# One table of node sums instead of two, with each store issued behind its predecessor

## What is computed

```python
# layer 0, per edge e and head h
scores = einsum(Q[dst], K[src] + 0.2 * rel[edge_type]) / 8
w = segment_softmax(scores, dst)
agg = segment_sum(w * V[src], dst)          # 12,500 x 4 x 64
x = layernorm(x + layernorm(agg @ Wo + bo + x) * gamma + beta)
# layer 1, edges and one self loop per node
xp = x @ W;  alpha = leaky_relu(a_src[src] + a_dst[dst])
w = segment_softmax(alpha, dst)
agg = segment_sum(xp[src] * w, dst)
out = layernorm(x + elu(agg + bias))
```

## Time and profile before

| | us |
|---|---|
| median of 3 runs | 4471.25 |
| lowest, highest | 4469.44, 4473.03 |
| profiled execution, span | 6181.0 |

### The profile page before, as it was taken

How to read it: one execution, slowest core, us unless ns; L and a number is a source line. 1 busy time by engine, 2 the same in 40 slices (tenths; PEclk the granted TensorE clock), 3 DMA queues, 4 the chain that set the end, 5 groups by cost and what they waited for, 6 DMA issues and landing times. The chain is left out here.

```text
span 6181.0 us, 164556 instructions
## 1 busy us (share of the span) xinstructions
PE 4261.5 (69%) x50798; PEld 2746.6 (44%) x50798; DVE 3295.8 (53%) x10527; ACT 2576.2 (42%) x6781; POOL 3049.7 (49%) x3229
## 2 busy tenths in 40 slices
PE   7958878777778787778786555555555555555554
PEld 4634444444444444444443444444444443444443
DVE  3235555555555555555554455555555555555555
ACT  2323344444444444444343444444444444444444
POOL 1245555545555555555452555555555555555553
PEclk9989999999999999999997666656566566565666
DMA  7856676666666666666664555555555555555554
GB/s 224 282 163 191 185 189 186 186 186 185 186 187 183 186 186 187 185 186 186 184 185 114 145 153 156 152 151 153 152 153 153 150 152 149 154 152 152 154 150 123
DMA packets 820553, 1055.91 MB, mean 171 GB/s; under 512 B 458633, under 2 KB 632338, under 8 KB 820464
## 3 DMA queue, kind: packets, MB, share of 16 engines
q0 software_dynamic: 225072, 730.03, 42.9%
q1 hardware_dynamic: 594078, 324.02, 20.6%
q10 hardware_dynamic: 1314, 0.99, 0.1%
HBM read 919.46 MB, written 133.59 MB: 170 GB/s over the span
## 5 line engine op out<-in xcount | busy, mean ns | idle before, releaser
L766 POOL DMA_INDIRECT typed_rows<-kv,typed_index x1563 | 1491.3, 954 | 1470.8 <-remote 570.5
L1298 POOL DMA_INDIRECT plain_rows<-xp,plain_index x1563 | 1486.0, 951 | 1359.5 <-remote 536.1
L875 PE MATMUL typed_p_s<-typed_kt,typed_q 64*32 64x416 f32 x4168 | 835.7, 549 | 336.6 <-issue 289.7
L997 DVE CUSTOM_DVE_ANT_0 typed_weight<-typed_p_s,typed_far 128x416 f32<-128x416 f32 x521 | 308.3, 592 | 1113.6 <-PE typed_p_s L875 1080.8
L1400 PE MATMUL plain_p_o<-plain_rows,plain_weight_t 128*32 128x65 f32 x16672 | 630.5, 296 | 331.5 <-issue 310.7
L1433 DVE SCALAR_TENSOR_TENSOR plain_p_s<-plain_p_s,plain_a_dst,plain_damped 128x416 f32<-128x416 f32 x521 | 342.3, 657 | 865.9 <-ACT plain_damped L1553 475.1
L1389 PE MATMUL plain_p_s<-all_cst,plain_rows 128*128 128x128 f32 x2084 | 546.2, 395 | 346.0 <-issue 319.6
L1375 PE MATMUL plain_p_w<-all_cst,plain_weight 128*128 128x128 f32 x1563 | 437.5, 404 | 431.6 <-issue 286.0
L1400 PEld LDWEIGHTS plain_p_o<-plain_rows,plain_weight_t 128*32 128x32 f32 x16672 | 459.2, 154 | 556.6 <-issue 516.7
L1167 ACT ACTIVATE typed_weight<-typed_weight,typed_col 128x416 f32<-128x416 f32 x521 | 334.7, 642 | 806.6 <-issue 549.7
L1389 PEld LDWEIGHTS plain_p_s<-all_cst,plain_rows 128*128 128x128 f32 x2084 | 406.0, 210 | 463.6 <-issue 437.6
(11 more groups left out here) (191 smaller groups left out, 6936.5 us busy)
## 6 DMA issues: line engine op xcount, KB each, us to landing
typed_match<-match SPq DMA_DIRECT2D x131, 208.0 KB
plain_match<-match SPq DMA_DIRECT2D x131, 208.0 KB
agg<-qkv_zero SPq DMA_DIRECT2D x98, 264.0 KB
typed_agg<-agg SPq DMA_DIRECT2D x98, 264.0 KB
plain_agg<-agg SPq DMA_DIRECT2D x98, 264.0 KB
kv<-qkv_kv SPq DMA_DIRECT2D x98, 258.0 KB
typed_kinds<-match SPq DMA_DIRECT2D x131, 192.0 KB
typed_rows<-kv,typed_index POOLq DMA_INDIRECT x1563
```

What stands on the lines that cost most here:

```text
L766: pool.indirect_dma_start(rows[:, r, j, :], None, k.kv, bass.IndirectOffsetOnAxis(ap=index[:, g, at:at + 1], axis=0)).then_inc(rows_in[r], 16)
L875: last = pe.matmul(p_s[at:at + TN, 0:SLOTS], q[own, m, :, h // 2], kt[own, h // 2, lo:lo + SLOTS], start=True, stop=True, tile_position=(H ...
L1298: pool.indirect_dma_start(rows[:, r, j, :], None, k.xp, bass.IndirectOffsetOnAxis(ap=index[:, g, at:at + 1], axis=0)).then_inc(rows_in[r], 16)
```

## The change

The table has one half. Tiles store to it in turn; from the second tile on, SyncE waits, behind the wait for the tile's result, until the store of the tile before has landed, and then issues the store. Rows that a tile doesn't own are so overwritten by the next tile. Nothing is zeroed but the 44 rows of nodes that don't exist (one DMA ahead of the loop). `load` fetches one half, 132 KB. VectorE's addition is gone in both layers. In layer 1 the block is fetched straight into `both`, and counts on the semaphore of the block's other load (`own_in`); its `load` now waits for `part_ready` of three blocks back instead of `joined` of the block before.

```diff
-        self.agg = dram("agg", (2, NP, HEADS, AG))
+        self.agg = dram("agg", (NP, HEADS, AG))
...
-            def clear(t):
-                sp.dma_start(k.agg[:, bass.ds(t.n * P, P)].rearrange("a n h c -> n a (h c)"), zero[:]).then_inc(zero_out, 16)
...
-            in_turn(sp, (0, load), (4, store), (0, clear))
-            sp.wait_ge(zero_out, 16 * ROWS)
+            sp.dma_start(k.agg[N:NP].rearrange("n h c -> n (h c)"), zero[0:NP - N]).then_inc(zero_out, 16)
+            in_turn(sp, (0, load), (4, store))
+            sp.wait_ge(zero_out, 16)
...
@@ put_out of layer 0, and the same lines in layer 1 @@
                 sp.wait_ge(result_ready, t.n + 1)
                 sp.sem_inc(slot_free, 1)
-                sp.dma_start(k.agg[t.slot(2), bass.ds(node, TN)].rearrange("n h c -> h n c"), result[:, m]).then_inc(result_out[m], 16)
+                if not t.known_below(1):
+                    before = t.back()
+                    sp.wait_ge(result_out[before.slot(4)], before.use(4) * 16 + 16)
+                    sp.sem_inc(slot_free, 1)
+                sp.dma_start(k.agg[bass.ds(node, TN)].rearrange("n h c -> h n c"), result[:, m]).then_inc(result_out[m], 16)
...
@@ load of layer 0 @@
-                sp.dma_start(agg[:], k.agg[:, bass.ds(b.n * P, P)].rearrange("a n h c -> n a (h c)")).then_inc(agg_in, 16)
+                sp.dma_start(agg[:], k.agg[bass.ds(b.n * P, P)].rearrange("n h c -> n (h c)")).then_inc(agg_in, 16)
...
@@ join of layer 0 @@
-                v.tensor_tensor(agg[:, 0], agg[:, 0], agg[:, 1], ALU.add).then_inc(joined, 1)
-                v.wait_ge(joined, b.n + 1)
...
@@ load of layer 1 @@
-                if not b.known_below(1):
-                    sp.wait_ge(joined, b.n)
-                sp.dma_start(agg[:], k.agg[:, bass.ds(b.n * P, P)].rearrange("a n h c -> n a (h c)")).then_inc(agg_in, 16)
+                if not b.known_below(GROUP):
+                    sp.wait_ge(part_ready, b.n - GROUP + 1)
+                sp.dma_start(both[:, o].rearrange("p h c -> p (h c)"), k.agg[bass.ds(b.n * P, P)].rearrange("n h c -> n (h c)")).then_inc(own_in[o], 16)
...
@@ join of layer 1 @@
-                v.wait_ge(agg_in, b.n * 16 + 16)
-                v.wait_ge(own_in[o], b.use(GROUP) * 16 + 16)
-                v.tensor_tensor(both[:, o].rearrange("p h c -> p (h c)"), agg[:, 0], agg[:, 1], ALU.add).then_inc(joined, 1)
+                v.wait_ge(own_in[o], b.use(GROUP) * 32 + 32)
...
-                v.wait_ge(joined, b.n + 1)
```

More of the change, by code:

```diff
@@ L531, in project_nodes @@
         beta = z.sb("beta", [P, D])
-        zero = z.sb("zero", [P, 2, HEADS * AG])
+        zero = z.sb("zero", [P, HEADS * AG])
         p_t = z.ps("p_t", [P, 2, 512])
@@ L711, in attend_typed @@
         gamma = z.sb("gamma", [P, D])
-        agg = z.sb("agg", [P, 2, HEADS * AG])
+        agg = z.sb("agg", [P, HEADS * AG])
         share = z.sb("share", [P, HEADS])
@@ L733, in attend_typed @@
         p_message, p_x1, p_out, p_1 = p_o[:, D:2 * D], p_t[:, 0:D], p_t[:, D:2 * D], p_n[:, 0:W1]
-        both = agg[:, 0].rearrange("p (h c) -> p h c", h=HEADS)
+        both = agg[:].rearrange("p (h c) -> p h c", h=HEADS)
         prod = kt[:, 0, 0:4 * D].rearrange("p (s a d) -> p s a d", s=2, a=2)
@@ L744, in attend_typed @@
             "scores_ready", "scored", "max_ready", "low_ready", "exp_done", "turned", "weight_t_ready", "agg_done", "result_ready"))
-        (weights_in, agg_in, row1_out, joined, share_ready, message_ready, message_t_ready, turned_both, moved, summed, stats1, moments1,
+        (weights_in, agg_in, row1_out, share_ready, message_ready, message_t_ready, turned_both, moved, summed, stats1, moments1,
          var1, root, inverse, centered, normed, stats2, moments2, var2, x1_ready, x1_t_ready, x1_kept, row1_ready,
          settled3, settled4, total_ready) = (z.sem(n) for n in (
-            "weights_in", "agg_in", "row1_out", "joined", "share_ready", "message_ready", "message_t_ready", "turned_both", "moved",
+            "weights_in", "agg_in", "row1_out", "share_ready", "message_ready", "message_t_ready", "turned_both", "moved",
             "summed", "stats1", "moments1", "var1", "root", "inverse", "centered", "normed", "stats2", "moments2", "var2", "x1_ready",
@@ L1278, in attend_plain @@
         settled4, keep_ready = z.sem("settled4"), z.sem("keep_ready")
-        (agg_in, joined, self_added, self_ready, empty_ready, top_ready, peak_ready, below_ready, scaled_ready, weighed, total_ready, whole_ready,
+        (self_added, self_ready, empty_ready, top_ready, peak_ready, below_ready, scaled_ready, weighed, total_ready, whole_ready,
          share_ready, self_done, part_ready, h_ready, grown_ready, kept_ready, y_ready, stats_ready, moments_ready, half_ready, root,
          res_ready, settled3) = (z.sem(n) for n in (
-            "agg_in", "joined", "self_added", "self_ready", "empty_ready", "top_ready", "peak_ready", "below_ready", "scaled_ready", "weighed",
+            "self_added", "self_ready", "empty_ready", "top_ready", "peak_ready", "below_ready", "scaled_ready", "weighed",
             "total_ready", "whole_ready", "share_ready", "self_done", "part_ready", "h_ready", "grown_ready", "kept_ready", "y_ready",
```

## The result

The changed kernel takes 4877.71 us (median of 4 runs, 4873.4 to 4895.56) against 4470.7 us of the kernel before beside it: 1.092 times as long, 95% interval 1.0907 to 1.0934, so 407 us slower. The forecast of 4461 us and its range up to 4560 us are both missed. What happened is the mechanism of the first rival, the chain of landings, but in both layers, and nearly six times as dear as its 68 us.

The account below looks back on a forecast made before the run. GpSimd's gathers, 3.75 us a tile, were taken to bound both loops at 3.82. With the wait hidden, 3.2 us of tails and 7 us of lateness, 10 us together, came off 4471.25: 4461 us, range 4430 to 4560.

Parts of the forecast that it names:

- the first rival: SyncE's wait ahead of the store sets layer 0's pace: L = 3.75 us, 68 us lost, 4535 us; chance 0.33.
- the added instructions: SyncE, both layers: a wait and a count, 0.2 us a tile, covered by 0.9 us; uncovered 208 us.
- the landing time L: SyncE's store, issue to landing: between 2.45 and 4.08 us, taken as 3.3; hidden if under 3.62 us.
- The brake: Layer 0: a slower loop loads the DMA engines less, hence L = 3.75 us and not 4.08.
- The rival's own upper case: Layer 0: with a landing time of 4.08 us the wait costs 240 us.
- the same sum stays under 3.6: Layer 1: landing time with one slab in four tiles and a DMA share of 0.58, under 3.6 us.
- a late landing is taken up by the lead: SyncE's fetches, both layers: two or three steps of lead absorb a single late landing; only the mean of L counts.
- The estimate that was set aside: Store landing by the Trainium skill's page: 2.45 + 1.8 = 4.25 us, the kernel some 330 us slower.
- A tenth of 78 us of lateness: Both loops: less VectorE work and less traffic remove a tenth of the time above the gathers' pace, 7 us.
- 3.2 us of tails: End of each layer: four VectorE additions fall away, 0.47 us each in layer 0, 0.34 in layer 1.
- the rival of the DMA engines: Layer 0: DMA engines set the pace, so halved block loads return 36 us, 4432 us with tails; chance 0.12.
- the wrong case: Signs of failure: SyncE waits a microsecond a tile for its own stores, TensorE or ScalarE wait, layer 0 longer.

Follow-up runs that it names:

- the second profile: The kernel before, unchanged, profiled a second time: a span of 4466.9 us, where its first profile had 6181.0 us.
- the run with two tiles back: Kernel before, plus a wait in both layers of each store for the store of two tiles back: 4468.93 us, ratio 1.0.
- after: The changed kernel with all of the change, against the kernel before: 4877.71 us, 1.092 times as long.

## Why the prediction failed, point by point

**The bound of before** was read rightly from a profile that didn't fit the runs: gathers at 3.82 us a tile were forecast for the runs, 3.88 and 3.77 came out; 486 us outside the loops, 349 + 77 + 53 = 479 in the second profile. That TensorE hides the zeroes, that the added instructions cost nothing (the run with two tiles back: 0, within 5 us) and that the halved loads win nothing were right.

**The step that failed is the landing time L.** It was bounded by 2.45 us and 4.08, and taken at 3.3. In the kernel before, undisturbed, L is 4.69 us in layer 0 and 3.96 in layer 1, above the upper end in the one layer and above the limit of 3.62 in both; under the chain itself it is 4.06 and 3.60. Both ends were made of the wrong things. The lower one came from the end of layer 1, where the gathers are done (a DMA share of 0.28 from 6144 to 6150 us); and what seemed to confirm it, the 1.5 us of waiting at the block loads, says little: the store they wait for has had the step's own store and fetches more in layer 0 and a whole step more in layer 1, and that profile lacks half of the events by which waits are found. The upper one added a slab in the queue, 0.7 us, whose place in the queue the two runs with another queue put at nothing, and one gather, 0.93 us, where half of the gathers' traffic alone takes 0.7 off. If the other half counts alike, an estimate from these two runs, gathers are 1.4 us of L: 2.45 + 1.4 = 3.85, near the 4.06 and 3.60 of after.

**The brake was named and under-sized.** The rival said that a slower loop loads the engines less, and took L = 3.75 for that. The share did fall (0.91 to 0.83) and L with it (4.69 to 4.06), but it settles there: 4.06 + 0.23 and a few late steps make 4.35. That the lower share is what shortens L is not shown apart: in the chain a store also never has the one before it still under way. The rival's own upper case, 240 us in layer 0, is about what that layer lost, 0.47 x 521 = 245 us; but its 4.08 us were added up from the wrong terms, so the match is luck.

**Layer 1 was waved through in one sentence**, "the same sum stays under 3.6". Undisturbed, L is 3.96 there, and 3.60 only under the chain. By the mean alone the layer would have lost little, 3.83 less 3.77, 0.06 us a tile. What failed besides is the step behind it, that a late landing is taken up by the lead and only the mean of L counts: a step in which SyncE's own list is longer than the landing adds to the chain. SyncE's step was put at 1.91 us and at most 2.9; the step with a block's loads, one in 5.3, takes 4.5 us and was not looked at. These steps are 0.25 us a tile, and with the 0.06 about the 0.29 of the layer.

**The estimate that was set aside was the better one.** By the Trainium skill, "DMA: Bandwidth & Descriptors", section "Latency and other measured facts" (a round trip to HBM of 2 us under high load), L had been estimated at 4.25 us and the loss at some 330. The traces agree in size for layer 0 (4.69 without the chain, 4.06 with it) and are below it in layer 1; the projection does not agree, with 2.45 us for stores at 281 GB/s. The 330 us were for layer 0 alone, which lost 245, so that they come near the 407 of both layers is luck. What had been set against the estimate, a load of 2.31 us at a share of 0.87, came from that stage, which has no gathers, and that it is a load is not the point: the kernel's own stores of zeros were a row of stores under that load, which the prediction held to be missing, and they would have misled it in the same way.

**The gain was under-sized too.** A tenth of 78 us of lateness and 3.2 us of tails were forecast, 10 us; the run without the wait is 26 us faster. By the difference of two runs it is the additions that bring it, not the traffic: the rival of the DMA engines, 36 us by freed traffic, falls with the run that has half the loads.

**Signs.** The signs of the wrong case came: waits of SyncE for its own stores of 743.5 / 521 = 1.4 and 0.95 us a tile, L783 (L785 before) gone from 439.5 to 20.6 us, ScalarE waiting for `a_dst`, a longer loop.

Left open: what sets the 3.84 to 3.90 us of layer 0 without the wait, above the gathers' 3.75 (in the second profile of before GpSimd waits 88.2 us for places in its ring there; what makes them late was not followed); and the part that TensorE's granted clock has (1.00 and 0.76 before, 0.95 and 0.71 after, in the stretches shown) now that TensorE waits more.

## What to carry to other kernels

A wait for the landing of the store before turns a stream of stores into a chain, and its price is landing time plus issue against the loop's step, at every step; the lead of several steps that the fetches had did not help here. Size that landing time in the stage where the chain will run and at the traffic of the undisturbed runs, not at a quiet end and not in a profile that is more than a third longer than the runs: VectorE's busy time carried over from that profile (3295.8 us, 3255.1 in the second), the time of a transfer didn't. And look at the longest of the issuing engine's steps, not only at the common one. Where order between neighbours can be loosened by one (two buffers, a wait two steps back), the same instructions cost nothing.

## What the runs showed of the hardware

The time of a 33 KB store from issue to semaphore went from 2.3 to 2.5 us (the shortest twentieth in after) to 4.69 us in the mean in layer 0 of the kernel before, at a DMA share of 0.91. The share alone doesn't set it: a 264 KB store took 2.45 us at 0.87 in the projection, where there are no gathers. Giving the stores, or the slabs ahead of them, another queue took nothing off in layer 0 (0.1 to 0.2 us were added) and 0.06 us at most in layer 1; halving the gathers of another queue changed it by 0.7. And the landing time of before overstates what a chain costs: (4.69 + 0.23 - 3.88) x 521 = 542 us in layer 0, against the 245 us that were lost, as stores under the chain land in 4.06 us. Whether that is the lower traffic of the longer loop or the one store less under way was not told apart.
